# Softmax maxima carried in two extra rows of the turned queries instead of a second accumulated matmul per score tile

## Chip, cores and metric

The kernel runs on one core of a Trainium2 chip. Its time is the device time of one execution in microseconds (us). The runs of the kernel before are given with their median, and one more execution was taken with the hardware profiler, which is where all rows below come from.

## What is computed

A two-layer network on 8 sequences of 256 tokens with 128 channels, in six stages: a mixture of 64 experts, an attention of 16 heads with 8 channels each (the first attention), the mixture again, a mixture of 8 experts, an attention of 16 heads with 64 channels, and that mixture again. Each stage normalises its input and adds its result to the residual. Only the first attention is changed. For a sequence of n = 256 tokens and 16 heads it is

```
q, k, v = split(x @ w_qkv.T + b_qkv)            # 16 heads, D = 8
q, k    = rope(elu(q) + 1), rope(elu(k) + 1)
attn    = softmax(einsum('bhnd,bhmd->bhnm', q, k) / sqrt(D), axis=-1)
out     = einsum('bhnm,bhmd->bhnd', attn, v) + depthwise_conv3(v)
```

## The kernel before

The stage is the function attention_zero (L1645 to L2197). Each engine has its own instruction list, which it works off in order; semaphores tie them together. TensorE is called PE here, VectorE DVE, ScalarE ACT, GpSimd POOL.

**Layout.** Queries and keys of a sequence are stacked by tokens (stack, L1687): for every head a strip of HW = 32 columns, of which PARTS = 24 hold the 8 channels three times, in parts (high, high, rest for q; high, rest, high for k), so that one product of 24 rows gives the score nearly in full precision; the other 8 are zero. PE turns the stack (turn_stack, L1901), four heads to 128 partitions, and ACT copies it to turned (take_stack, L2056): head h lies in partitions 32*(h%4) and up.

**Two products of the same scores.** scores_by_query (L1940) gives a head's scores with queries on partitions, in bank 0 or 1, and DVE reduces them to negated maxima (maximum, L2123). scores_by_key (L1961) gives the same scores with keys on partitions, in banks 2 to 5, two heads at a time, and ACT takes their exponential (probabilities, L2072), which the product with the values needs in this layout (values, L1984, 16 matmuls L1997 for four heads). A softmax's maximum belongs to a query, which here lies along the free dimension, so it can't be a bias of ACT. Before, it is added by PE: each score tile is accumulated from a product of 24 rows (L1974) and a second one of 32 rows in bf16 (L1980), of shift, which holds the turned maxima of all heads in two bf16 parts, with select, a matrix of ones and zeros that picks the head's two rows.

**The maxima's way.** split_maxima (L2131) writes the 16 maxima of each of the two token tiles in two bf16 parts, four times over (mparts, 128 columns for a token tile); turn_maxima (L1952) turns them with 2 bf16 transposes (L1956) into bank T = 7; take_shift (L2141) copies them (L2145) to shift.

**Order of work.** The loops run over steps n = 8*i + u, i the sequence, u = 0 to 7. Step n multiplies by key the heads 2u and 2u+1 of sequence i, and multiplies by query two heads that come 11 steps later (units, L1751): the maxima of sequence i+1 are complete at u = 4, split at u = 5, turned at u = 6 and copied at u = 7. PE's order in a step (L2009 to L2039): scores_by_key; the first of the two heads by query; at odd n the values, at even n turn_out (L2001); at u = 0 values_and_convolution of the next sequence (L1918); at u = 1 to 4 one turn_stack; at u = 6 turn_maxima; at u = 7 project of sequence i+4 (L1884, only while i+4 < 8); the second head by query. So PE meets at each border of steps a block of 12 matmuls: 2 by query (the second head of the step before), 8 by key, 2 by query. DVE's order (L2175 to L2195): at u = 5 split_maxima, at u = 1 add_convolution, at u = 7 take_shift; the first maximum; at u = 0 elus (L2109); finish (even n) or take_out (odd n); the second maximum. A product by query waits for the maximum two heads back, as only two banks serve it.

**Bank T** is shared: turn_stack, turn_maxima, project and values_and_convolution take turns in it, each waiting until the one before has been read (claim, L1879). project of u = 7 waits for take_shift of u = 7; values_and_convolution at u = 0 waits for elus, which waits for ACT's exponentials of project's result.

```
1959:             release[T] = (shift_ready, b + 1)
```

Of the kernel before, what the change touches and what calls it, by code (L numbers as in the profile page):

```python
# [14 lines left out]
BF16 = mybir.dt.bfloat16  # L15
# [8 lines left out]
P = 128  # L24
BATCH = 8
SEQ = 256
# [1618 lines left out]
def attention_zero(core, name, ctx, w):  # L1645
# [9 lines left out]
    HW = 32  # L1655
    PARTS = 3 * D0
    STEPS = H0 // 2
# [23 lines left out]
    head = sb("head", [P, H0], BF16)  # L1681
    select = sb("select", [P, H0, P], BF16)
# [8 lines left out]
    mparts = sb("mparts", [P, 2, 4, 2 * H0], BF16)  # L1691
    shift = [sb(f"shift{i}", [P, SEQ], BF16) for i in range(2)]
# [12 lines left out]
    head_ready = sem("head_ready")  # L1705
    rows_done = sem("rows_done")
    rows_ready = sem("rows_ready")
    select_ready = sem("select_ready")
# [81 lines left out]
    def stacks(eng, b, step):  # L1790
        s = b % 2
        q, k = (stack[s][:, a, :, :, :].rearrange("p t h d -> p (t h) d") for a in range(2))
        for a, m in enumerate((q, k)):
            full = z[s][:, 2 * a:2 * a + 2, :].rearrange("p t (h d) -> p (t h) d", d=D0)

            view = m[:, :, 0:PARTS].rearrange("p n (i d) -> p n i d", d=D0)
# [3 lines left out]
        for a, m in enumerate((q, k)):  # L1800
            full = z[s][:, 2 * a:2 * a + 2, :].rearrange("p t (h d) -> p (t h) d", d=D0)
            at = 2 * D0 if a == 0 else D0
            last = rest_part(eng, m[:, :, at:at + D0], full, m[:, :, 0:D0])
        return last

    def gpsimd(pool):
# [16 lines left out]
        for m in stack:  # L1823
            pool.memset(m[:, :, :, :, PARTS:HW].rearrange("p a t h d -> p (a t h) d"), 0.0).then_inc(filled, 1)
        step(pool.memset(head[:, :], 0.0))

        for part in range(2):
            ins = pool.affine_select(out=head[:, :].rearrange("p (g j) -> p g j", j=HG),
                                     in_=head[:, :].rearrange("p (g j) -> p g j", j=HG), compare_op=ALU.not_equal,
                                     fill=1.0, base=-H0 * part, pattern=[[-HG, GROUPS], [-HW - 1, HG]],  # L1830
                                     channel_multiplier=1)
            if part == 0:
                step(ins)
        ins.then_inc(head_ready, 1)
# [41 lines left out]
    def tensor(pe):  # L1876
# [24 lines left out]
        def turn_stack(b, v):  # L1901
# [4 lines left out]
            if b == 0 and v == 0:  # L1906
                pe.wait_ge(filled, 3)
# [10 lines left out]
        def values_and_convolution(b):  # L1918
            i = value_bank(b)
            claim(i)  # L1920
            if b == 0:
                pe.wait_ge(v_prep_ready, 1)
                pe.wait_ge(filled, 5)
# [16 lines left out]
        def scores_by_query(b, h):  # L1940
            n, g, rows = b * H0 + h, h // HG, slice(HW * (h % HG), HW * (h % HG) + PARTS)
# [10 lines left out]
        def turn_maxima(b):  # L1952
            claim(T)
            pe.wait_ge(parts_ready, b + 1)
            for t in range(2):
                last = pe.transpose(bank[T].bitcast(BF16)[:, P * t:P * t + P],  # L1956
                                    mparts[:, t, :, :].rearrange("p i h -> p (i h)"), core.identb[:, :])
# [3 lines left out]
        def scores_by_key(b, u):  # L1961
            m = b * STEPS + u
            if m == 0:
                pe.wait_ge(select_ready, 1)
# [790 lines left out]
```

## Time and profile before

| | us |
|---|---|
| median of 3 runs | 1109.68 |
| lowest and highest | 1099.80, 1115.09 |
| the profiled execution, its own time | 1098.92 |
| its span in the profile | 1097.2 |

The span runs from the first to the last instruction of the core; the execution's own time is 1.7 us longer. The profile lists for each engine how long it was busy, and a granted clock of TensorE of 1.0 (2.4 GHz) or 0.5 (1.2 GHz) by stretch. In the timeline, instructions of one line that follow each other closely are merged ("x2"), and the time in brackets is the engine's idle time before, with what ended it. A matmul's recorded duration holds its latency, so successive starts, not durations, tell its pace. The first attention lies between 133.7 and 335 us.

### The profile page before, as it was taken

The numbers are of one execution on the slowest core, as the hardware profiler recorded it, in microseconds if no ns is written. First come the engines' busy times: TensorE is split into PE (matmuls) and PEld (weight loads), VectorE is DVE, ScalarE is ACT, GpSimd is POOL, SyncE is SP. The second block draws the span as 40 slices with busy tenths as digits, with TensorE's granted clock in tenths as the row PEclk, the third lists the DMA queues.
The fourth block names the chain that finished last, engine by engine and source line by source line (L and its number), as shares of the span: only waits on it lengthen the run. The fifth ranks groups of instructions, "written<-read, shape, count | busy, mean of one in ns | idle before, by whom it ended". The sixth has DMA issues, their size and how long they took to land.

```text
span 1097.2 us, 23131 instructions
## 1 busy us (share of the span) xinstructions
PE 914.0 (83%) x7238; PEld 688.1 (63%) x7242; DVE 757.6 (69%) x2659; ACT 534.7 (49%) x1489; POOL 272.2 (25%) x349
## 2 busy tenths in 40 slices
PE   5899758999996899937997289999999999658992
PEld 4466646666764456836896166666666766437992
DVE  7767885787868766885555557677677667674555
ACT  4222132665664232034454258677778668523553
POOL 1012183323101004047744410000000000067642
PEclk9999965999996999957999589999999999958997
DMA  9031099600006212083311175534643541253303
GB/s 243 19 98 34 16 364 328 206 2 1 1 2 169 55 41 90 1 249 99 106 42 40 56 211 174 149 113 125 193 116 98 174 135 59 62 153 92 91 32 118
DMA packets 134947, 119.47 MB, mean 109 GB/s; under 512 B 11011, under 2 KB 115227, under 8 KB 134836
## 3 DMA queue, kind: packets, MB, share of 16 engines
q1 hardware_dynamic: 130292, 109.57, 33.9%
q0 software_dynamic: 4544, 8.54, 2.4%
q8 instruction: 55, 0.90, 0.3%
q14 instruction: 56, 0.46, 0.1%
HBM read 67.19 MB, written 51.80 MB: 108 GB/s over the span
## 4 chain that ended last, share of the span: by engine, by line
PE 58%; DVE 21%; issue 9%; DMA 3%; ACT 3%; POOL 3%; SPq 1%; DVEq 1%; POOLq 0%; ACTq 0%
PE psum L802 5%; PE psum L1374 5%; PE psum L1292 4%; PE psum L811 4%; PE psum L1948 4%; PE psum L1997 3%; PE psum L590 3%; PE psum L2418 3%; PE psum L2463 3%; PE psum L2430 2%; DVE a_L L2588 2%; PE psum L592 2%; PE psum L591 2%; DVE a_G L2507 2%; PE psum L1912 2%
## 5 line engine op out<-in xcount | busy, mean ns | idle before, releaser
L2128 DVE TENSOR_REDUCE a_negmax<-psum 128x2 f32<-128x512 f32 x128 | 84.4, 687 | 36.4 <-PE psum L1948 35.6
L2077 ACT ACTIVATE a_PT<-psum 128x1024 f32<-128x1024 f32 x64 | 65.6, 1025 | 28.5 <-PE psum L1980 28.3
L2534 ACT ACTIVATE a_pr<-a_L,a_least 128x128 f32<-128x128 f32 x128 | 50.8, 397 | 54.1 <-DVE a_least L2588 54.1
L857 ACT ACTIVATE f_hT<-psum,f_wt 128x128 f32<-128x128 f32 x156 | 44.7, 369 | 46.8 <-PE psum L802 46.8
L857 ACT ACTIVATE g_hT<-psum,g_wt 128x128 f32<-128x128 f32 x156 | 44.5, 370 | 44.7 <-PE psum L802 40.9
L1948 PE MATMUL psum<-a_turned 24*128 24x256 f32 x256 | 59.3, 355 | 5.7 <-DVE a_negmax L2128 5.7
L2536 ACT ACTIVATE a_pr<-a_L,a_least 128x256 f32<-128x256 f32 x128 | 63.7, 498 | 0.0
L2418 PE MATMUL psum<-a_KT,a_Q 64*128 64x128 f32 (+1 forms) x512 | 59.7, 351 | 1.4 <-DVE a_least L2588 1.4
L2453 PEld LDWEIGHTS psum<-a_PT,a_V 128*64 128x64 f32 x512 | 31.0, 136 | 40.9 <-issue 16.8
L2544 ACT ACTIVATE a_PT<-psum 128x384 f32<-128x384 f32 x128 | 55.6, 489 | 1.9 <-PE psum L2430 1.7
L2430 PE MATMUL psum<-ident,a_pr 128*128 128x128 f32 x384 | 53.6, 276 | 2.9 <-DVE a_pr L2354 2.6
L2453 PE MATMUL psum<-a_PT,a_V 128*64 128x256 f32 (+1 forms) x512 | 55.5, 338 | 0.0
L2588 DVE CUSTOM_DVE_ANT_0 a_L<-psum,a_X 128x256 f32<-128x256 f32 x128 | 53.8, 421 | 0.0
L1974 PE MATMUL psum<-a_turned 24*128 24x256 f32 x256 | 53.0, 349 | 0.0
L1948 PEld LDWEIGHTS psum<-a_turned 24*128 24x128 f32 x256 | 39.1, 203 | 21.0 <-DVE a_negmax L2128 10.1
L576 POOL CAST a_xs_high<-a_xnT 128x256 fp32r<-128x256 f32 x8 | 3.3, 417 | 194.4 <-PE psum L592 194.4
L946 DVE COPY g_wt<-g_w_all 128x1156 f32 x39 | 29.9, 769 | 30.6 <-DVE g_y L940 27.0
L946 DVE COPY f_wt<-f_w_all 128x1156 f32 x39 | 30.6, 786 | 28.8 <-DVE f_y L940 25.4
L2586 DVE CUSTOM_DVE_ANT_0 a_L<-psum,a_X 128x128 f32<-128x128 f32 x128 | 36.7, 286 | 18.5 <-PE psum L2418 18.5
L2430 PEld LDWEIGHTS psum<-ident,a_pr 128*128 128x128 f32 x384 | 44.3, 141 | 7.8 <-issue 2.7
L802 PE MATMUL psum<-f_xT,f_wt 128*128 128x128 f32 x312 | 47.3, 298 | 1.3
L743 POOL DMA_INDIRECT g_back_dram<-g_y,g_xin x39 | 40.1, 1029 | 32.3 <-DVE g_y L940 28.5
(574 smaller groups left out, 2687.6 us busy)
## 6 DMA issues: line engine op xcount, KB each, us to landing
z<-a_G SPq DMA_DIRECT2D x32, 512.0 KB, 2.9
a_X<-z SPq DMA_DIRECT2D x16, 1024.0 KB, 7.0
f_slots_dram<-empty SPq DMA_DIRECT2D x1, 8910.0 KB, 27.1
g_slots_dram<-empty SPq DMA_DIRECT2D x1, 8910.0 KB, 51.1
a_X<-z SPq DMA_DIRECT2D x16, 512.0 KB, 3.9
f_wgu<-in_gate_up SPq DMA_DIRECT2D x16, 384.0 KB, 6.3
z<-pad SPq DMA_DIRECT2D x6, 1024.0 KB, 10.3
g_wgu<-in_gate_up SPq DMA_DIRECT2D x16, 384.0 KB, 7.0
```

The source lines that it names most:

```text
L802: last = pe.matmul(bank[i % 2][:, P * c:P * c + P], wt[i % WBUF][:, P * c:P * c + P], xT[:, i % 2, :], start=True, stop=True)
L857: act.activation(hT[:, i % 2, c, :], bank[i % 2][:, P * c:P * c + P], ACT.Relu, bias=wt[i % WBUF][:, B1 + c:B1 + c + 1]).then_inc(relu_don ...
L946: dve.tensor_copy(wt[i % WBUF][:, :], w_all[:, ds(e, 1), :].rearrange("p a n -> p (a n)")).then_inc(copied, 1)
L1948: last = pe.matmul(bank[h % 2][:, SEQ * t:SEQ * t + SEQ], q[rows, g, P * t:P * t + P].bitcast(F32R), k[rows, g, :].bitcast(F32R), start=Tr ...
L2077: act.activation(PT[m % 4][:, :, :, :].rearrange("p j t n -> p j (t n)"), core.psum[:, 2 + 2 * (u % 2):4 + 2 * (u % 2), :], ACT.Exp, scale ...
L2128: dve.tensor_reduce(negmax[:, :, h], bank[h % 2].rearrange("p (t n) -> p t n", n=SEQ), AX.X, ALU.max, negate=True).then_inc(max_done, 1)
L2418: last = pe.matmul(out, Q[s][rows, c, queries], KT[s][rows, c, keys], start=True, stop=True)
L2430: last = pe.transpose(bank[2 + i][:, P * j:P * j + P], pr[:, n % SLOTS, P * j:P * j + P], core.ident[:, :])
L2453: last = pe.matmul(o[D1 * i:D1 * i + D1, queries], V[s][:, kt, D1 * h:D1 * h + D1], PT[:, (2 * m + i) % TSLOTS, keys], start=(kt == 0), st ...
L2536: act.activation(pr[:, o, P:3 * P], L[:, o, P:3 * P], ACT.Exp, bias=least[:, o, 1:2], scale=-1.0, accum_out=sums[:, o, 1:2]).then_inc(p_re ...
L2544: act.activation(PT[:, n % TSLOTS, :], bank[2 + n % 2][:, 0:3 * P], ACT.Copy).then_inc(pT_ready, 1)
L2588: dve.tensor_tensor_reduce(L[:, o, P:3 * P], S[:, P:3 * P], X1[s][:, h, :], 1.0, 3.0e38, ALU.add, ALU.min, least[:, o, 1:2]).then_inc(l_re ...
```

## The change

The strip of a head gets two rows ahead of its 24: USED = OWN + PARTS = 26 of 32. In the keys they are ones, in the queries zeros, so that the product by query is what it was. When the maxima are known they are turned to where each head's two rows lie, with zeros elsewhere, and added in place to the turned queries; the product by key then holds them, and the second accumulation goes, with select, shift and the head pattern they were made from. mparts grows to four groups of 128 columns, turn_maxima to 8 transposes, and take_shift becomes an addition over 4 groups of 256 columns.

```diff
@@ -1652,8 +1652,10 @@
     bank = core.bank
     SCALE = float(1.0 / np.sqrt(D0))
-    HW = 32
+    HW, OWN = 32, 2
     PARTS = 3 * D0
+    USED = OWN + PARTS
     STEPS = H0 // 2
     GROUPS = H0 // HG
...
@@ -1688,8 +1688,8 @@
     turned = [[sb(f"turned{i}{a}", [P, GROUPS, SEQ]) for a in range(2)] for i in range(NT)]
     Vs = [sb(f"Vs{i}", [P, 2, H0, VW]) for i in range(NT)]
     negmax = sb("negmax", [P, 2, H0])
-    mparts = sb("mparts", [P, 2, 4, 2 * H0], BF16)
-    shift = [sb(f"shift{i}", [P, SEQ], BF16) for i in range(2)]
+    mparts = sb("mparts", [P, 2, GROUPS, HG * HW], BF16)
     PT = [sb(f"PT{i}", [P, 2, 2, SEQ]) for i in range(4)]
     OT = [sb(f"OT{i}", [P, SEQ]) for i in range(2)]
     rden = sb("rden", [P, 2, HG])
...
@@ -1793,14 +1792,14 @@
-            view = m[:, :, 0:PARTS].rearrange("p n (i d) -> p n i d", d=D0)
+            view = m[:, :, OWN:USED].rearrange("p n (i d) -> p n i d", d=D0)
...
-            last = rest_part(eng, m[:, :, at:at + D0], full, m[:, :, 0:D0])
+            last = rest_part(eng, m[:, :, OWN + at:OWN + at + D0], full, m[:, :, OWN:OWN + D0])
...
@@ -1821,17 +1820,10 @@
         pool.memset(ones_f[:, :], 1.0).then_inc(diag_ready, 1)
         pool.memset(ln.xnT[:, :, 0:SEQ + 2:SEQ + 1], 0.0).then_inc(filled, 1)
         for m in stack:
-            pool.memset(m[:, :, :, :, PARTS:HW].rearrange("p a t h d -> p (a t h) d"), 0.0).then_inc(filled, 1)
-        step(pool.memset(head[:, :], 0.0))
-
-        for part in range(2):
-            ins = pool.affine_select(out=head[:, :].rearrange("p (g j) -> p g j", j=HG),
-                                     in_=head[:, :].rearrange("p (g j) -> p g j", j=HG), compare_op=ALU.not_equal,
-                                     fill=1.0, base=-H0 * part, pattern=[[-HG, GROUPS], [-HW - 1, HG]],
-                                     channel_multiplier=1)
-            if part == 0:
-                step(ins)
-        ins.then_inc(head_ready, 1)
+            for a, ones in enumerate((0.0, 1.0)):
+                pool.memset(m[:, a, :, :, 0:OWN].rearrange("p t h d -> p (t h) d"), ones).then_inc(filled, 1)
+            pool.memset(m[:, :, :, :, USED:HW].rearrange("p a t h d -> p (a t h) d"), 0.0).then_inc(filled, 1)
+        pool.memset(mparts[:, :, :, :], 0.0).then_inc(mparts_filled, 1)
         pool.wait_ge(bias_loaded, 16)
         step(pool.tensor_copy(bias[:, 0:2, :], bqkv[:, 0:2, :]))
         split_bias(0, 2, qk_bias_ready)
...
@@ -1938,7 +1930,7 @@
             release[i] = (l_added, b + 1)
         def scores_by_query(b, h):
-            n, g, rows = b * H0 + h, h // HG, slice(HW * (h % HG), HW * (h % HG) + PARTS)
+            n, g, rows = b * H0 + h, h // HG, slice(HW * (h % HG), HW * (h % HG) + USED)
             if h % (2 * HG) == 0:
                 pe.wait_ge(tk_ready, 4 * b + 2 * (h // (2 * HG)) + 2)
             if n >= 2:
...
@@ -1952,16 +1944,15 @@
         def turn_maxima(b):
             claim(T)
             pe.wait_ge(parts_ready, b + 1)
-            for t in range(2):
-                last = pe.transpose(bank[T].bitcast(BF16)[:, P * t:P * t + P],
-                                    mparts[:, t, :, :].rearrange("p i h -> p (i h)"), core.identb[:, :])
+            for g in range(GROUPS):
+                for t in range(2):
+                    last = pe.transpose(bank[T].bitcast(BF16)[:, SEQ * g + P * t:SEQ * g + P * t + P], mparts[:, t, g, :],
+                                        core.identb[:, :])
             last.then_inc(parts_turned, 1)
             release[T] = (shift_ready, b + 1)
         def scores_by_key(b, u):
             m = b * STEPS + u
-            if m == 0:
-                pe.wait_ge(select_ready, 1)
             if u == 0:
                 pe.wait_ge(shift_ready, b + 1)
             if m >= 2:
...
@@ -1970,15 +1961,10 @@
             for t in range(2):
                 for j in range(2):
                     h = 2 * u + j
-                    rows = slice(HW * (h % HG), HW * (h % HG) + PARTS)
-                    pe.matmul(bank[2 + 2 * (u % 2) + j][:, SEQ * t:SEQ * t + SEQ],
-                              k[rows, h // HG, P * t:P * t + P].bitcast(F32R), q[rows, h // HG, :].bitcast(F32R),
-                              start=True, stop=False, skip_group_check=True)
-                for j in range(2):
-                    h = 2 * u + j
-                    rows = slice(HW * (h % HG), HW * (h % HG) + HW)
-                    last = pe.matmul(bank[2 + 2 * (u % 2) + j][:, SEQ * t:SEQ * t + SEQ], select[rows, h, :],
-                                     shift[b % 2][rows, :], start=False, stop=True, skip_group_check=True)
+                    rows = slice(HW * (h % HG), HW * (h % HG) + USED)
+                    last = pe.matmul(bank[2 + 2 * (u % 2) + j][:, SEQ * t:SEQ * t + SEQ],
+                                     k[rows, h // HG, P * t:P * t + P].bitcast(F32R), q[rows, h // HG, :].bitcast(F32R),
+                                     start=True, stop=True, skip_group_check=True)
             last.then_inc(s2_done, 1)
         def values(m):
...
@@ -2079,8 +2065,6 @@
         ln.deviation(act)
         act.activation(ln.unused[:, 1:2], core.ones[:, 0:1], ACT.Exp)
-        act.wait_ge(head_ready, 1)
-        copy(select[:, :, :], bcast(head[:, :], P)).then_inc(select_ready, 1)
         ln.take_quarter(act, 0)
         for n in range(FIRST, END):
             i, u = place(n)
...
@@ -2132,17 +2116,19 @@
             dve.wait_ge(max_done, H0 * (b + 1))
             if b:
                 dve.wait_ge(parts_turned, b)
-            full = negmax[:, :, :].unsqueeze(2).to_broadcast([P, 2, 4, H0])
-            dve.tensor_copy(mparts[:, :, :, 0:H0], full).then_inc(hi_ready, 1)
+            else:
+                dve.wait_ge(mparts_filled, 1)
+            own = mparts[:, :, :, :].rearrange("p t g (j c) -> p t (g j) c", c=HW)
+            dve.tensor_copy(own[:, :, :, 0], negmax[:, :, :]).then_inc(hi_ready, 1)
             dve.wait_ge(hi_ready, b + 1)
-            dve.tensor_tensor(mparts[:, :, :, H0:2 * H0], full, mparts[:, :, :, 0:H0],
-                              ALU.subtract).then_inc(parts_ready, 1)
+            dve.tensor_tensor(own[:, :, :, 1], negmax[:, :, :], own[:, :, :, 0], ALU.subtract).then_inc(parts_ready, 1)
         def take_shift(b):
             dve.wait_ge(parts_turned, b + 1)
-            if b >= 2:
-                dve.wait_ge(s2_done, STEPS * (b - 1))
-            dve.tensor_copy(shift[b % 2][:, :], bank[T].bitcast(BF16)[:, 0:SEQ]).then_inc(shift_ready, 1)
+            q = turned[b % NT][0]
+            dve.tensor_tensor(q[:, :, :].bitcast(F32R), q[:, :, :], bank[T].bitcast(BF16).rearrange("p (g n) -> p g n", n=SEQ),
+                              ALU.add).then_inc(shift_ready, 1)
         def add_convolution(b):
```

The waits for filled count the four more memsets, and the declarations of head, select and their semaphores go.

## Rows read from the trace of the kernel before

**Rows 1.** The page: busy time, share of the span, instructions.
```profile
PE 914.0 (83%) x7238; PEld 688.1 (63%) x7242; DVE 757.6 (69%) x2659; ACT 534.7 (49%) x1489; POOL 272.2 (25%) x349
```

**Rows 2.** Stretches of the first attention: us, each engine's busy time, granted clock, DMA.
```profile
227.24:232.08 4.84, 3.73 (x32) 3.14 (x31) 3.25 (x6) 2.14 (x3) 2.34 (x3) 1.00 0.00 0
232.08:238.81 6.73, 6.73 (x84) 4.57 (x83) 5.43 (x12) 4.55 (x6) 4.42 (x6) 1.00 0.02 5
...
227.24:247.60 20.36, 19.25 (x209) 14.01 (x208) 16.17 (x37) 11.88 (x15) 6.76 (x8) 1.00 0.01 2
```

**Rows 3.** Timeline of PE from block of step 5: start, us, idle before.
```profile
240.53 0.38 PE L1948 MATMUL psum<-a_turned 24*128 24x256 f32 x1
...
241.45 1.07 PE L1997 MATMUL psum<-a_PT,a_Vs 128*32 128x256 f32 x16
242.45 0.38 PE L1948 MATMUL psum<-a_turned 24*128 24x256 f32 x1
...
243.31 0.50 PE L1948 MATMUL psum<-a_turned 24*128 24x256 f32 x2
...
244.02 0.27 PE L1956 MATMUL psum<-identb,a_mparts 128*128 128x128 bf16 x2
```

**Rows 4.** Timeline of DVE over steps 4 to 7 of the same sequence.
```profile
239.35 1.29 DVE L2128 TENSOR_REDUCE a_negmax<-psum 128x2 f32<-128x512 f32 x2 [0.56 <-PE psum L1948]
...
245.94 0.28 DVE L2145 COPY a_shift<-psum 128x256 bf16<-128x256 bf16 x1
...
246.73 0.42 DVE L2158 COPY a_OT<-psum 128x256 f32<-128x256 f32 x1
```

**Rows 5.** Timeline of PE and DVE across the end of that sequence.
```profile
246.31 0.70 PE L1894 MATMUL psum<-a_wqkv,a_xnT 128*128 128x256 f32 x2
...
247.60 0.38 PE L1948 MATMUL psum<-a_turned 24*128 24x256 f32 x1
...
248.14 1.29 DVE L2128 TENSOR_REDUCE a_negmax<-psum 128x2 f32<-128x512 f32 x2 [0.99 <-PE psum L1948]
...
249.34 0.68 DVE L2114 SCALAR_TENSOR_TENSOR a_elu<-psum,a_e 128x512 f32<-128x512 f32 x1
...
250.08 0.70 PE L1928 MATMUL psum<-a_wv,a_xnT 128*128 128x256 f32 x2 [1.12 <-DVE a_elu L2114]
```

**Rows 6.** Groups by line and shape, 140 to 330 us: busy us, mean ns, idle before.
```profile
L1980 PE MATMUL psum<-a_shift,a_select 32*128 32x256 bf16 x256 | 46.5, 282 | 0.0
...
L2138 DVE TENSOR_TENSOR a_mparts<-a_negmax,a_mparts 128x128 bf16<-128x128 f32 x8 | 2.3, 292 | 0.3
...
L2136 DVE CAST a_mparts<-a_negmax 128x128 bf16<-128x128 f32 x8 | 1.8, 227 | 0.3
```

**Rows 7.** Timeline of the last steps, without products by query: PE.
```profile
326.39 0.38 PE L1974 MATMUL psum<-a_turned 24*128 24x256 f32 x2
...
326.62 0.28 PE L1980 MATMUL psum<-a_shift,a_select 32*128 32x256 bf16 x2
...
326.87 0.28 PE L1980 MATMUL psum<-a_shift,a_select 32*128 32x256 bf16 x2
...
329.17 0.38 PE L1974 MATMUL psum<-a_turned 24*128 24x256 f32 x2
```

**Rows 8.** Single lines: durations in ns min/median/max, first and last start, shapes.
```profile
L2151 DVE TENSOR_TENSOR x<-x,psum x8: 410/410/414, 181.5 to 309.5; 128x256 f32<-128x256 f32 x8
...
L2114 DVE SCALAR_TENSOR_TENSOR a_elu<-psum,a_e x8: 678/682/692, 146.8 to 269.7; 128x512 f32<-128x512 f32 x8
...
L1788 POOL TENSOR_TENSOR a_z<-a_z,a_rot x6: 1270/1281/1282, 170.4 to 273.4; 128x512 f32<-128x512 f32 x6
```

**Rows 9.** Timeline ahead of the first block by key: PE's project.
```profile
183.36 0.70 PE L1894 MATMUL psum<-a_wqkv,a_xnT 128*128 128x256 f32 x2 [0.30 <-DVE a_shift L2145]
```

**Rows 10.** Stretches: the first block by key up to the next, and the stage after.
```profile
184.80:191.88 7.08, 5.66 (x29) 4.83 (x28) 1.98 (x3) 2.25 (x3) 3.86 (x4) 0.54 0.58 198
191.30:338.00 146.70, 136.43 (x1526) 97.03 (x1525) 111.15 (x276) 86.29 (x104) 32.88 (x43) 1.00 0.14 42
```

## What the change does to the time, predicted before it was run

> **What bounds the kernel now.** The page comes first: PE is the busiest engine over the whole span, DVE the second [rows 1]. That average covers six stages, and only the first attention changes, so the next view is the stretches of that stage. It is periodic: one sequence of eight steps takes 20.36 us, of which PE is busy 19.25 and DVE 16.17 [rows 2]. The reader should see two kinds of stretch in it. From the block of step 1 (232.08) to that of step 4 (238.81) PE is busy 6.73 of 6.73 us and DVE 5.43: PE sets the pace. From step 0 to step 1 PE is busy only 3.73 of 4.84 us [rows 2]. The third view, DVE's timeline, tells what happens between: from 239.35 DVE works without a gap until the end of the copy that starts at 246.73 and takes 0.42, so for 7.8 us DVE sets the pace [rows 4]. PE's timeline agrees: the block of step 6 starts at 242.45, and its last pair by query only at 243.31, having waited for a maximum [rows 3]. Last, the end of a sequence: project at 246.31, right behind take_shift (245.94 + 0.28 = 246.22) [rows 4, 5]; the block of step 0 at 247.60; DVE's maximum at 248.14 after 0.99 us of idleness; elus at 249.34; values_and_convolution at 250.08, for which PE idled 1.12 us [rows 5].
>
> So a sequence is a ring of four parts: PE's steps 1 to 3; DVE from step 4 to take_shift; project and the block of step 0; the wait for elus and values_and_convolution. A saving counts only in the part whose engine sets the pace.
>
> **Removed: four bf16 matmuls per step**, 256 in all [rows 6]. Their mean of 282 ns is latency, not pace. A block of twelve matmuls takes 0.92 us from its first start to the next operation (240.53 to 241.45) [rows 3]. In the last steps, which have no product by query, a pair of 24-row products plus a pair of bf16 ones takes 0.25 us (bf16 start at 326.62 to the next bf16 start at 326.87) [rows 7]. Both kinds stream 256 columns, so about half of it, 0.11 to 0.12, belongs to the bf16 pair. A block has two such pairs: 0.22 us less, leaving 0.70. Bounds: nothing, if the other row groups' streams keep the block as long, and 0.31, if a third of it goes as four of twelve instructions. I take 0.22, as the two rows in the last steps measure the pair itself.
>
> In steps 1 to 3 that is 3 x 0.22 = 0.66 us, if DVE keeps up. DVE idles 0.56 us once in two steps (the bracket at 239.35) [rows 4], and two steps would lose 0.44. That nearly exhausts its slack, and the second step of a pair will sometimes wait. I take 0.5 us per sequence. In steps 4 to 7 DVE sets the pace: nothing. In step 0 the maximum comes 0.54 us after the block starts, from its first two matmuls (247.60 to 248.14) [rows 5], and then DVE's two maxima and elus follow each other: nothing.
>
> **Moved and grown: take_shift.** The copy of 256 columns took 0.28 us [rows 4]. It becomes an fp32 addition of 1024 columns, one operand from PSUM. Not in the trace; the nearest rows are the DVE operations with one PSUM and one SBUF operand: 410 ns for 256 columns, 682 for 512 [rows 8]. That is 1.0625 ns a column, hence 682 + 512 x 1.0625 = 1226 ns, 0.94 more. Bounds: 0.68 in all, if it took no longer than 512 columns do; 2.55, if it ran at POOL's 1.28 us per 512 [rows 8]. I take 1.23, the straight line through DVE's own rows.
>
> **Split of the maxima.** A cast of 227 ns and a subtraction of 292 over 128 columns [rows 6] become the same over 32 columns. Estimate: 0.15 + 0.20, 0.17 us less; bounds 0 and 0.25. It is in DVE's unbroken stretch, so it counts.
>
> **Turning.** Eight transposes instead of two. The two take 0.27 us and one lasts 0.22 (mean pace 0.05 to 0.06) [rows 3], so six more cost PE 0.33 us at step 6. There PE waits for DVE (0.86 us into its block at 243.31) [rows 3], which hides them. If that cover were gone, they would cost 0.33 per sequence.
>
> **The wait that grows.** project claims bank T and may start only when take_shift has read it. take_shift would end at 246.22 - 0.17 + 0.94 = 246.99, project at about 247.05 instead of 246.31: 0.75 us later [rows 4, 5]. Behind it in PE's order stand the last product by query and the block of step 0; DVE's maxima, elus and values_and_convolution wait for these. ACT's exponentials too are 0.75 later, in step with the rest. On DVE the maximum and take_out behind take_shift (1.0 us) fall into the idle 0.99 us before 248.14, which moves along with PE [rows 5].
>
> **The rest.** ACT's copy of select goes, once, at the start, where ACT waits for PE's transposes right after: nothing. POOL's extra memsets replace two selects and have slack: nothing, at most 0.5. Waits on shift buffers go; they weren't late.
>
> **The sum**, against the profiled execution's own time of 1098.92 us:
> - sequences 0 to 3 (with project): -0.5 + 0.75 = +0.25 each, +1.0.
> - sequences 4 to 6: no project, but take_shift still stands ahead of the maximum that frees a bank; +0.2 each, +0.6.
> - before the first block by key: project already waits there for take_shift (0.30 us) [rows 9], so +0.94, and 0.1 for transposes at the low clock: +1.0.
> - the last eleven steps have no maxima. Two take 2.78 us (326.39 to 329.17) [rows 7]; the blocks give 0.5, but values, DVE's copy, turning back and DVE's division, which share one bank, need almost as long. I take 0.15 per pair, -0.6 with the odd ends; bounds -0.2 and -2.5.
>
> Together +2.0 us: 1100.9 on the profiled execution's scale. The median of the runs shown stands 10.8 us above that execution, so the forecast for a median is 1109.7 + 2.0 = 1111.7 us. A measurement of this kernel tells about 2% (22 us) from no change, and all of this is far below.
>
> **Rivals.**
> 1. PE sets the pace throughout. For it: PE busy 19.25 of 20.36 us [rows 2]. Against it: DVE's 7.8 us without a gap [rows 4]. It gives 64 x 0.22 = 14.1 less and 7 x 0.33 = 2.3 more: -11.8, 1097.9 us. Chance 0.15.
> 2. The addition is much dearer than the line through DVE's rows. At the upper bound of 2.55 it costs 1.32 more on each of 8 turns: 1111.7 + 10.6 = 1122.3 us. For it: a bf16 PSUM operand mixed with an fp32 one is in no row. Against it: no DVE row is that slow per column. Chance 0.1.
> 3. The removal doesn't do what it says: the bf16 pairs stream beside products of other row groups and the block keeps nearly 0.92. Then the 0.5 per sequence doesn't come: 6 sequences x 0.5 = 3.0 more, 1114.7 us. For it: the block overlaps four row groups already, twelve matmuls in 0.92 us [rows 3]. Chance 0.1.
> 4. Slower, by the clock. PE gets idler: 0.75 us more before project, shortly before its idle 1.12 us [rows 5]. If the granted clock falls at each end of a sequence, that stretch costs what it did the first time, at a mean clock of 0.54: 7.08 us instead of 4.84 [rows 2, 10], 2.24 each. With seven sequences: +15.7, 1127.4 us. It decides from the point where the two idle stretches together look to the chip like those before 191 us. Against it: from 191.3 to 338 us the clock stayed at 1.00, through idle stretches of 1.12 us [rows 5, 10]. Chance 0.1.
>
> On the fourth, the Trainium skill, "TensorE: Matmul & The Clock Gate", section "Part 4: PE-mode transpose", says that transposes don't count as PE activity for the clock as other matmuls do. This change removes counted matmuls and adds transposes, so by that page its chance would be higher. The trace speaks against a large effect: the clock was full through stretches with many transposes.
>
> **Chances.** The forecast has 0.5, the four rivals 0.15, 0.1, 0.1, 0.1, and 0.05 is left for what I don't see. The range takes in the first three rivals, and the spread of the runs before: 1097 to 1124 us. The fourth lies outside. Faster by over 2% needs more than all the PE work removed: 0.02. Slower by over 2% needs the clock to fall and the addition to be dear as well: 0.04. Within 2%: 0.94.
>
> **What would show it.** Right: in the profile after, the addition at about 1.23 us; the block near 0.70 us; project waiting about 0.8 us for take_shift; the last steps slightly shorter; a sequence of 20.4 to 20.8 us; DVE's busy time up by some 6 us in the stage and PE's down by about 10. Wrong: a sequence under 20 us (rival 1), the addition above 1.5 us (rival 2), the block still near 0.9 (rival 3), a granted clock of 0.5 between 191 and 338 us (rival 4).

## The result, and the profile after

| | before | after |
|---|---|---|
| median of 20 executions, us | 1105.14 | 1113.89 |
| lowest and highest | 1096.34, 1115.73 | 1107.84, 1117.69 |
| mean | 1106.5 | 1113.4 |
| the profiled execution, own time | 1098.92 | 1112.25 |

The ratio after to before is 1.0096, with a 95% interval of 1.0069 to 1.0124; this ratio and those below leave out executions more than 1.5% above the fastest of their kernel. Over all 20 executions of each, the means differ by 6.9 us (0.6%) and the medians by 8.7. So the kernel got slower by 0.6 to 1%. The forecast of 1111.7 us lies 2.2 us below the median, but its step was +2.0 us.

The three runs known before hid a pattern. Of the 20 executions before, ten lie at 1096.3 to 1100.7 us and ten at 1109.6 to 1115.7, with nothing between. Of the 20 after, none is below 1107.8. The profile before is of the lower group.

The page after, to set beside [rows 1]:

```profile
PE 920.4 (83%) x7030; PEld 689.2 (62%) x7034; DVE 765.2 (69%) x2659; ACT 531.6 (48%) x1488; POOL 273.2 (25%) x351
```

PE has 208 instructions fewer (256 removed, 48 added) and is nevertheless busy 6.4 us longer. Fewer instructions that are busy for longer are the first sign of the clock. The stretches of the first attention, with the granted clock in the third place from the end, answer to [rows 2, 10]:

```profile
184.40:194.60 10.20, 8.59 (x36) 7.11 (x37) 2.49 (x5) 2.52 (x4) 4.77 (x6) 0.50 0.70 227
...
198.10:215.20 17.10, 17.10 (x114) 10.98 (x112) 10.89 (x23) 7.05 (x9) 0.00 (x0) 0.50 0.77 231
...
218.60:222.00 3.40, 3.40 (x18) 3.10 (x16) 0.76 (x1) 0.00 (x0) 3.32 (x4) 0.50 0.02 5
222.00:297.10 75.10, 66.86 (x688) 47.80 (x692) 62.35 (x139) 44.22 (x57) 23.07 (x29) 1.00 0.01 1
297.10:303.90 6.80, 6.80 (x38) 5.25 (x31) 4.31 (x9) 1.78 (x2) 0.00 (x0) 0.50 0.02 4
...
237.82:258.55 20.73, 18.11 (x184) 12.99 (x184) 17.03 (x37) 11.78 (x15) 6.75 (x8) 1.00 0.01 2
```

Before, PE ran at 2.4 GHz from 191.3 to 338 us without a break [rows 10]. After, it is at 1.2 GHz until 194.6, again from 198.1 for 17.1 us, and twice more. At full clock (last row) a sequence takes 20.73 us instead of 20.36; PE is busy 18.11 of it instead of 19.25 and DVE 17.03 instead of 16.17 [rows 2].

That gives a balance, from the starts of ACT's 64 exponentials. The first and the last, before (L2077) and after (L2063):

```profile
186.53 1.02 ACT L2077 ACTIVATE a_PT<-psum 128x1024 f32<-128x1024 f32 x1 [0.36 <-PE psum L1980]
...
329.96 1.02 ACT L2077 ACTIVATE a_PT<-psum 128x1024 f32<-128x1024 f32 x1
...
188.16 1.01 ACT L2063 ACTIVATE a_PT<-psum 128x1024 f32<-128x1024 f32 x1
...
343.60 1.03 ACT L2063 ACTIVATE a_PT<-psum 128x1024 f32<-128x1024 f32 x1
```

The last one starts 13.6 us later than before. The first starts 1.6 later; the sequences 2, 3, 4 and 6, without a fall of the clock, take 0.37, 0.37, 0.35 and 0.36 us more; sequences 0, 1 and 5, with falls, take 7.0, 1.9 and 2.1 more; the last steps take 0.5 less. Sum: 13.6. If the three had cost 0.37 each, 3.7 us would be left. So between these two executions **3.7 us is the ring of waits, and 9.9 us is the clock that fell where it had not fallen before**. The 3.7 hold some more of the clock: the 1.6 us at the start include 1.0 that project lost by running at 1.2 GHz. Against the kernel before as a whole the clock's share is smaller, because the profile before is of the group that kept its clock: if the 3.7 us hold in the means too, 3.2 of their difference of 6.9 are left for the clock (an estimate).

The ring looks as the prediction drew it. DVE's timeline over steps 5 to 7, to [rows 4]:

```profile
231.22 0.24 DVE L2122 CAST a_mparts<-a_negmax 128x32 bf16<-128x32 f32 x1
231.49 0.30 DVE L2124 TENSOR_TENSOR a_mparts<-a_negmax,a_mparts 128x32 bf16<-128x32 f32 x1
...
235.26 1.21 DVE L2130 TENSOR_TENSOR a_turned<-a_turned,psum 128x1024 fp32r<-128x1024 f32 x1
```

PE's, of the same sequence, to [rows 3, 5]:

```profile
233.34 0.61 PE L1949 MATMUL psum<-identb,a_mparts 128*128 128x128 bf16 x8
...
236.52 0.70 PE L1886 MATMUL psum<-a_wqkv,a_xnT 128*128 128x256 f32 x2 [0.82 <-DVE a_turned L2130]
...
237.82 0.38 PE L1940 MATMUL psum<-a_turned 26*128 26x256 f32 x1
...
238.48 0.44 PE L1990 MATMUL psum<-ident,a_OT 128*128 128x128 f32 x2
...
240.29 0.70 PE L1920 MATMUL psum<-a_wv,a_xnT 128*128 128x256 f32 x2 [1.38 <-DVE a_elu L2098]
```

The addition lasts 1.21 us. project starts 0.05 after its end, having waited 0.82 us. The block of step 0 takes 0.66 (237.82 to 238.48), where the block of [rows 3] took 0.92. And before values_and_convolution PE idles 1.38 us instead of 1.12: the quarter of a microsecond that the block lost went into the wait, as forecast for step 0.

### The profile page after: what moved, and what is told of

Same layout as the page of the kernel before. It is cut to its first block, busy times and chain, and to the rows that moved or that the text cites. A ratio compares the mean times of both kernels' runs of the same rounds, so it can differ in the third digit from the quotient of the medians.

```text
span 1110.4 us, 22707 instructions
## 1 busy us (share of the span) xinstructions
PE 920.4 (83%) x7030; PEld 689.2 (62%) x7034; DVE 765.2 (69%) x2659; ACT 531.6 (48%) x1488; POOL 273.2 (25%) x351
## 4 chain that ended last, share of the span: by engine, by line
PE 55%; DVE 25%; issue 9%; DMA 3%; ACT 3%; DVEq 2%; SPq 1%; POOL 1%; POOLq 0%; ACTq 0%
PE psum L802 6%; PE psum L1374 5%; PE psum L811 4%; PE psum L1292 4%; PE psum L2404 3%; PE psum L590 3%; PE psum L2449 3%; PE psum L1940 3%; DVE a_negmax L2112 2%; PE psum L2416 2%; PE psum L1983 2%; DVE a_L L2574 2%; PE psum L592 2%; PE psum L591 2%; DVE a_G L2493 1%
## 5 line engine op out<-in xcount | busy, mean ns | idle before, releaser
L2063 ACT ACTIVATE a_PT<-psum 128x1024 f32<-128x1024 f32 x64 | 65.2, 1023 | 28.4 <-PE psum L1965 27.7
L1940 PE MATMUL psum<-a_turned 26*128 26x256 f32 x256 | 52.3, 372 | 7.6 <-DVE a_negmax L2112 7.3
L1940 PEld LDWEIGHTS psum<-a_turned 26*128 26x128 f32 x256 | 33.2, 216 | 25.1 <-DVE a_negmax L2112 18.5
L743 POOL DMA_INDIRECT f_back_dram<-f_y,f_xin x39 | 40.5, 1039 | 30.4 <-DVE f_y L940 25.7
L1965 PE MATMUL psum<-a_turned 26*128 26x256 f32 x256 | 47.3, 323 | 0.5 <-DVE a_turned L2130 0.4
```

The lines of the kernel that those rows point to most:

```text
L743: pool.indirect_dma_start(back_dram[:, :], bass.IndirectOffsetOnAxis(ap=xin[:, i, P:P + 1].bitcast(I32), axis=0), y[i % YBUF][:, :], None, ...
L1940: last = pe.matmul(bank[h % 2][:, SEQ * t:SEQ * t + SEQ], q[rows, g, P * t:P * t + P].bitcast(F32R), k[rows, g, :].bitcast(F32R), start=Tr ...
L2063: act.activation(PT[m % 4][:, :, :, :].rearrange("p j t n -> p j (t n)"), core.psum[:, 2 + 2 * (u % 2):4 + 2 * (u % 2), :], ACT.Exp, scale ...
```

## Experiments

Two theories. **Ring**: the loss is the longer chain DVE, project, DVE, values. **Clock**: PE, with less to do and more to wait for, is granted 1.2 GHz more often, and most of the loss is that. Beside each kernel stand 29 executions of the kernel before on the same chip. The chips differ: means of the kernel before are 1140.4 us (first chip), 1141.5 (second) and 1107.7 (third), so each kernel is read against its own. Means here are over all executions, and the clock is the granted clock of an execution, averaged over them. The standard error of a difference between two of these means is 1.4 to 2.5 us. Each kernel has one profile, of one of its executions.

| kernel | chip | executions | mean us | against before | mean clock | full-clock sequence us |
|---|---|---|---|---|---|---|
| before | first | 29 | 1140.4 | | 0.891 | 20.36 |
| no_second | first | 12 | 1149.5 | +9.1 | 0.878 | 19.81 |
| long_shift | first | 6 | 1154.1 | +13.8 | 0.887 | 21.6 |
| filler | first | 12 | 1144.8 | +4.4 | 0.890 | 20.73 |
| early_add | first | 12 | 1146.9 | +6.5 | 0.883 | 20.13 |
| before | second | 29 | 1141.5 | | 0.890 | 20.36 |
| changed_again | second | 6 | 1153.0 | +11.5 | 0.879 | 20.73 |
| zero_pairs | second | 12 | 1146.2 | +4.8 | 0.892 | 21.29 |
| before_filler | second | 12 | 1138.3 | -3.2 | 0.893 | 20.36 |
| by_query_first | second | 12 | 1145.5 | +4.0 | 0.885 | 19.89 |
| before | third | 29 | 1107.7 | | 0.896 | 20.36 |
| before_reordered | third | 12 | 1103.5 | -4.2 | 0.901 | 20.29 |
| changed_padded | third | 12 | 1107.2 | -0.5 | 0.900 | 20.07 |
| changed_unpadded | third | 12 | 1104.4 | -3.4 | 0.900 | 19.91 |

The sequence is the time between exponentials of two sequences' same step, where the clock was full between; for the kernel before it is from its one profile.

### The removal alone: no_second

```diff
-                              start=True, stop=False, skip_group_check=True)
-                for j in range(2):
...
-                    last = pe.matmul(bank[2 + 2 * (u % 2) + j][:, SEQ * t:SEQ * t + SEQ], select[rows, h, :],
-                                     shift[b % 2][rows, :], start=False, stop=True, skip_group_check=True)
+                              start=True, stop=True, skip_group_check=True)
```

> The kernel before without its 256 bf16 matmuls; all else stays, the copy of the turned maxima too, so the scores by key are not lowered by their maxima. It is the removal alone. Theory 'ring': blocks of 0.68 us instead of 0.92, but only the three blocks of steps 1 to 3 count: 0.4 to 0.5 us less per sequence, 2 to 4 us less in all against the kernel before. Theory 'clock': the same shortening, but with less for PE to do the granted clock falls in early sequences in more of the executions, so the median comes out 0 to 6 us above the kernel before, at a mean clock of 0.89 to 0.90.

Measured: ratio 1.0073 (1.0027 to 1.012). From the exponential of one step 1 to the next it takes 19.81 us instead of 20.36, so the ring got 0.55 us shorter, a little more than the 0.4 to 0.5 expected. Yet the kernel is 9.1 us slower in the mean and 15.0 in the median, more than even theory clock gave. Its twelve executions lie at 1144.3 to 1153.6 us, at clocks of 0.875 to 0.883. The kernel before on this chip has 17 at 1132.9 to 1138.4 (clock 0.889 to 0.903) and 12 at 1147.1 to 1150.0 (0.879 to 0.886). The stretches of no_second:

```profile
198.80:215.90 17.10, 17.10 (x109) 10.61 (x108) 10.09 (x23) 7.20 (x9) 0.00 (x0) 0.50 0.87 264
...
253.40:267.10 13.70, 12.77 (x65) 9.21 (x67) 6.56 (x15) 3.58 (x6) 4.68 (x5) 0.50 0.00 0
...
297.80:308.00 10.20, 10.20 (x61) 7.75 (x61) 5.34 (x14) 2.61 (x4) 0.00 (x0) 0.50 0.00 1
```

Work was only taken away, nothing put on DVE, no wait added, and the kernel lost time at the lower clock. Theory ring can't give that.

### DVE's part alone: long_shift

```diff
         def take_shift(b):
...
+            dve.tensor_tensor(spare[:, :, :].bitcast(F32R), turned[b % NT][0][:, :, :],
+                              bank[T].bitcast(BF16)[:, 0:SEQ].unsqueeze(1).to_broadcast([P, GROUPS, SEQ]), ALU.add)
             dve.tensor_copy(shift[b % 2][:, :], bank[T].bitcast(BF16)[:, 0:SEQ]).then_inc(shift_ready, 1)
```

> The kernel before with one more DVE addition of 1024 fp32 columns ahead of take_shift's copy, its result unused: DVE's part of the change alone (1.13 us more per sequence, where the change has 0.93), with all matmuls kept. Theory 'ring': project starts 1.1 us later, each sequence about 1.05 us longer, 7 to 8.5 us in all. Theory 'clock': the same plus a fall of the granted clock in early sequences, 12 to 18 us in all.

Measured: ratio 1.0104 (1.0034 to 1.0174), +13.8 in the mean, in the range of theory clock, at a mean clock of 0.887 against 0.891. A sequence grew by 1.28 us (21.64), somewhat more than expected. PE's timeline has the wait:

```profile
239.66 0.70 PE L1895 MATMUL psum<-a_wqkv,a_xnT 128*128 128x256 f32 x2 [1.03 <-DVE a_shift L2148]
```

So DVE's work ahead of project does pass into the ring nearly whole, as the prediction had it. In the profile the clock fell to 1.2 GHz for 20.5 us here too, though all PE work was kept:

```profile
199.20:219.70 20.50, 20.50 (x135) 13.12 (x134) 11.76 (x25) 7.98 (x10) 0.00 (x0) 0.50 0.64 193
```

But this run doesn't separate the theories. The interval, 4 to 20 us, also holds what theory ring gives for 1.28 us in each of seven sequences, 9 us. And the profile is of the slowest of the six (clock 0.877); the other five have 0.885 to 0.891, inside the range of the kernel before. That an added wait alone lets the clock fall is not shown.

### Work put back where it isn't needed: zero_pairs, beside changed_again

changed_again is the changed kernel, unedited. zero_pairs:

```diff
...
+                for j in range(2):
+                    h = 2 * u + j
+                    rows = slice(HW * (h % HG), HW * (h % HG) + HW)
+                    last = pe.matmul(bank[2 + 2 * (u % 2) + j][:, SEQ * t:SEQ * t + SEQ], zeros[rows, 0:P],
+                                     zeros[rows, :], start=False, stop=True, skip_group_check=True)
```

> The changed kernel as it is, beside the runs of the kernel before on the same chip as the three that follow. Both theories: about 1% above the kernel before in the mean; sequences of 20.72 us where the clock is full. Theory 'clock': executions of the kernel before fall in two clusters 13 to 15 us apart, by their mean granted clock, and those of the changed kernel all lie at a clock as low as the upper cluster's. Theory 'ring': the changed kernel shows the same two clusters, each some 4 us up.

> The changed kernel with the 256 bf16 matmuls put back at their old places, of the same shape, multiplying zeros, so that they add nothing to the scores. PE has the work of before and DVE that of the change. Theory 'ring': strictly more work than the changed kernel: blocks of 0.92 us again, some 0.5 us more per sequence, 3 to 4 us above the changed kernel. Theory 'clock', in the form that the removal of PE work lets the clock fall: mean granted clock higher by 0.005 to 0.01 than the changed kernel's, and the time equal to or 2 to 8 us below it, in spite of the added work.

Measured: changed_again 1.012 (1.0054 to 1.0186), zero_pairs 1.0044 (1.0004 to 1.0085). zero_pairs does all that the changed kernel does and 256 matmuls more. At full clock its sequence is 0.56 us longer, as theory ring says. It is 6.8 us faster in the mean (standard error 2.1; changed_again has only six executions), at a clock of 0.892 against 0.879. Its executions lie at 1143.8 to 1149.0, those of changed_again at 1147.8 to 1160.9. The stretches of changed_again:

```profile
185.50:195.70 10.20, 8.65 (x37) 7.17 (x38) 2.32 (x4) 2.52 (x4) 4.97 (x6) 0.50 0.70 225
...
199.10:216.20 17.10, 17.10 (x114) 10.98 (x112) 10.85 (x23) 7.00 (x9) 0.00 (x0) 0.50 0.77 230
...
298.10:304.90 6.80, 6.80 (x39) 5.25 (x31) 4.28 (x9) 1.75 (x2) 0.00 (x0) 0.50 0.01 4
```

And those of zero_pairs, whose first falls end at 196.8 us and which then has one short one:

```profile
186.60:196.80 10.20, 8.78 (x41) 7.23 (x40) 2.23 (x4) 2.63 (x4) 5.01 (x6) 0.50 0.71 227
196.80:258.30 61.50, 55.59 (x613) 40.19 (x610) 50.14 (x107) 35.18 (x44) 16.15 (x20) 1.00 0.27 79
258.30:261.70 3.40, 3.40 (x19) 3.10 (x18) 0.40 (x1) 0.39 (x1) 3.26 (x5) 0.50 0.00 0
```

changed_again repeats the falls of the first profile on another chip, nearly to the microsecond, so they aren't an accident of one execution. It is the fastest of its six; the others, up to 13 us longer at clocks down to 0.869, have no profile. In the profile of zero_pairs the long fall is gone. The two kernels differ only in unneeded work, and the one with more is faster at a higher clock. Theory ring had it 3 to 4 us slower. Measured against the 6.9 us of the changed kernel's first 20 executions instead of the 11.5, zero_pairs still stands 2 us lower, not 3 to 4 higher. So putting the matmuls back wins more by the clock than it costs in the ring. The second half of what was expected of changed_again by theory clock holds too: no execution at the lower group's clock of 0.894 to 0.900. The first half, "about 1%", was 1.2%.

### Idle stretches filled: filler and before_filler

```diff
+        def filler(n, first, many):
+            if n < 0:
+                claim(first)
+            else:
+                pe.wait_ge(p_ready, n)
+            for _ in range(many):
+                pe.matmul(bank[first], ones_f[:, :].bitcast(F32R), bias_rows[:, 0:4, :].bitcast(F32R), start=True,
+                          stop=True, skip_group_check=True)
...
+            if 0 <= n and value_step(n) is not None:
+                filler(n, 4, 4)
             if value_step(n) is not None:
                 values_and_convolution(value_step(n))
...
+            if -1 <= n and u == 7 and inside(i + 4):
+                filler(n, 2, 3)
             if u == 7 and inside(i + 4):
                 project(i + 4)
```

before_filler has the first call only, with 5 matmuls, in the kernel before.

> The changed kernel, with extra matmuls whose results nobody reads, issued by PE just where it would idle: 3 of 512 columns ahead of project at each step 7, 4 ahead of values_and_convolution at each step 0, from the first block by key on. They add nothing to the work that is used. Theory 'clock' (about 4 us of the change's loss is the ring of waits, the rest is a granted clock that falls in the first two sequences because PE idles more): the clock stays up more often, the mean granted clock of a run rises from 0.89 towards 0.91, and the time falls by 5 to 10 us below the changed kernel's. Theory 'ring' (the whole loss is the longer chain DVE, project, DVE, values): the time stays within 2 us of the changed kernel's, or rises by 1 to 2 us where a filler runs over.

> The kernel before with 5 unread matmuls of 512 columns at each step 0, where PE idles 1.12 us before values_and_convolution; nothing else. Theory 'ring': the same time or up to 1 us more. Theory 'clock': the cluster of slow executions (mean clock 0.88, 14 us longer) gets rarer or goes, and the mean falls by 3 to 6 us, the lowest execution staying within 1 us.

Measured: filler 1.0058 (1.0018 to 1.0099), before_filler 0.9988 (0.9948 to 1.0027). The cleaner of the two is before_filler. Its ratio doesn't tell it from the kernel before; the distribution of its executions does. Of 29 executions of the kernel before, 15 lie at 1132.4 to 1136.8 and 14 at 1146.9 to 1152.2. With the fillers the twelve lie at 1136.6 to 1140.2: the upper group is gone, and the mean is 3.2 us lower for more work. Against what was expected, the lowest rose by 4.2 us instead of 1. PE's timeline shows the fillers fit (the product behind them starts without a wait):

```profile
230.43 1.41 PE L2014 MATMUL psum<-a_bias_rows,a_ones_f 128*128 128x512 f32 x5
231.79 0.70 PE L1928 MATMUL psum<-a_wv,a_xnT 128*128 128x256 f32 x2
```

but only while there are elus to wait for. Sequences 5 and 6, which have none, took 18.92 and 15.94 us instead of 17.76 and 14.77, 2.3 us together for nothing.

filler, on the changed kernel, has fillers at the same two places and still stands only 4.4 us above its kernel before, where the changed kernel stands 6.9 and 11.5 above on its two chips. It ran on another chip than changed_again, so its gain is less sure. It fell short of what theory clock gave: the clock did not rise towards 0.91 but stayed at 0.890, and the gain is 2.5 or 7 us, by which of the two it is set against, where 5 to 10 were expected. In its profile, of its fastest execution, the clock stays up from 192.8 to 308.9 us, and sequence 0 takes 22.05 us instead of 28.6:

```profile
192.80:308.90 116.10, 110.42 (x1067) 78.98 (x1069) 94.11 (x208) 66.48 (x85) 31.47 (x38) 1.00 0.17 51
```

### Shorter rings: early_add and by_query_first

```diff
-            if u == 7 and inside(i + 1):
-                take_shift(i + 1)
...
+            if u == 6 and inside(i + 1):
+                take_shift(i + 1)
             if due[1]:
                 maximum(*due[1])
```

> The changed kernel, with take_shift moved on DVE from the head of step 7 to ahead of the second maximum of step 6, so that one maximum of 0.60 us no longer stands between the turned maxima and the release of bank T. Theory 'ring': each sequence with project gets 0.5 to 0.6 us shorter (20.72 to about 20.15), those without somewhat less, 3 to 4 us in all against the changed kernel. Theory 'clock': the same 3 to 4 us, and if the idle time before project is what lets the clock fall, 5 us or more on top, as the mean granted clock rises above 0.90.

by_query_first adds to that, on PE:

```diff
+            if 0 <= n and u == 0 and due[1]:
+                scores_by_query(*due[1])
             if value_step(n) is not None:
                 values_and_convolution(value_step(n))
...
-            if due[1]:
+            if due[1] and not (0 <= n and u == 0):
                 scores_by_query(*due[1])
```

> early_add, and at step 0 the second head's product by query goes ahead of values_and_convolution instead of behind it, so that PE does it in its idle 1.38 us and DVE reduces it while PE is at the convolution. Both theories: a sequence shorter by 0.2 to 0.4 us than early_add's 20.13. Theory 'ring': 1.5 to 3 us below early_add in all. Theory 'clock': PE's idle stretch is cut by 0.4 us, so the clock falls a little less often, and the time is 3 us or more below early_add's.

Measured: early_add 1.0051 (1.0003 to 1.0099), by_query_first 1.0063 (1.0025 to 1.0101). Both shorten the ring as worked out: 20.13 us (0.60 less, by the one maximum that no longer stands in the way) and 19.89 (0.24 less). In early_add the addition ends at 246.29 and project waits 0.23 instead of 0.82:

```profile
245.08 1.21 DVE L2130 TENSOR_TENSOR a_turned<-a_turned,psum 128x1024 fp32r<-128x1024 f32 x1
...
246.35 0.70 PE L1886 MATMUL psum<-a_wqkv,a_xnT 128*128 128x256 f32 x2 [0.23 <-DVE a_turned L2130]
```

Both rings are shorter than that of the kernel before, and both kernels are slower than it, at clocks of 0.883 and 0.885. Two of early_add's twelve, the profiled one among them, kept a clock of 0.891 and 0.894 and took 1137 to 1138 us; the other ten took 1145 to 1156. by_query_first stands 2.5 us lower against its own kernel before than early_add does, within the 1.5 to 3 of theory ring and short of the 3 or more of theory clock. The further hope of theory clock, that the idle time ahead of project is what lets the clock fall, didn't come true: most of it went, and the clock stayed at 0.883. A shorter ring for the same work doesn't by itself keep the clock up. zero_pairs, with the pairs of zeros, held 0.892 and filler 0.890, the level of the kernel before.

### A version that beats both?

before_reordered is the kernel before with the order of by_query_first at step 0 and 1 + 3 fillers around it, only for sequences 0 to 4. changed_unpadded is by_query_first with the same fillers. changed_padded has the pairs of zeros as well, only at steps 5, 6, 7 and 0.

```diff
+            if 0 <= n and u == 0 and i + 3 < BATCH:
+                filler(n, 4, 1)
             if 0 <= n and u == 0 and due[1]:
                 scores_by_query(*due[1])
+            if 0 <= n and u == 0 and i + 3 < BATCH:
+                filler(n, 4, 3)
...
```

> The kernel before with two edits at step 0 of sequences 0 to 4, where PE idles 1.12 us: the second product by query goes ahead of values_and_convolution (as in by_query_first), and 1 + 3 unread matmuls of 512 columns fill most of the rest; no fillers where there are no elus (before_filler had them there too, and its sequences 5 and 6 grew by 1.1 us each). Theory 'clock': no slow cluster, all executions within some 5 us, the mean 5 to 7 us below the mean of the kernel before, and the lowest executions 1 to 2 us below its lowest by the reordering (0.2 to 0.3 us a sequence). Theory 'ring' alone: both clusters stay, each 1 to 2 us lower.

> The changed kernel with the addition early, the second product by query first at step 0, the same 1 + 3 fillers at step 0 of sequences 0 to 4, and the bf16 matmuls with zeros put back only at steps 5, 6, 7 and 0 of sequences 0 to 6, where DVE sets the pace. Theory 'clock': the pairs are nearly free there (sequences within 0.2 us of by_query_first's 19.9) and the clock stays up as in the kernel before: 4 to 8 us below the mean of the kernel before. Theory 'ring' alone: the time of by_query_first, 4 us above the mean of the kernel before.

> changed_padded without the bf16 matmuls with zeros: addition early, second product by query first, fillers at step 0. It tells the pairs of zeros at DVE's steps from the fillers at step 0. Theory 'clock': the filled idle stretch alone brings back part of it: mean granted clock between by_query_first's and changed_padded's, and the time 2 to 4 us above changed_padded. Theory 'ring' alone: 0 to 1 us below changed_padded, as it has less work.

Measured: ratios 0.9994 (0.9954 to 1.0034), 0.998 (0.9932 to 1.0028) and 1.0009 (0.9965 to 1.0053). None is told from the kernel before by its interval. Over all executions before_reordered is 4.2 us below its mean and at most 1107.2 us, where 16 of the 29 of the kernel before are above 1108.9. changed_unpadded is 3.4 below in the mean, changed_padded 0.5. So the change can be kept at no loss, with the addition early, the order of step 0 turned and its idle time filled, but it brings nothing over the same fillers without it. Of what was expected, before_reordered came near: no execution in the upper group but two levels still, its mean 4.2 below and not 5 to 7, its lowest no lower (1098.7 against 1098.2). changed_padded missed its 4 to 8 us: two of its twelve lie at 1116.5. changed_unpadded was expected 2 to 4 us above changed_padded and came out 2.9 below, with a standard error of 1.7: the pairs of zeros show no gain once the fillers are there (clocks of 0.900 and 0.900), and cost 0.16 us per sequence. The reordering in the kernel before gave 0.07 us per sequence, not 0.2 to 0.3.

## Why the prediction was right and wrong

- **The number**: near the median by luck. The base was the median of three executions, 1109.7 us, 4.5 above the 1105.1 of twenty, which fall in two groups; the step was 6.7 too small, +2.0 instead of +8.7. The two errors nearly cancel.
- **Which engine sets the pace where**: right. A block shrank by 0.26 us (0.22 was taken). In a whole sequence the removal alone gives 0.55 (0.5 was taken), not the 8 x 0.22 of rival 1.
- **The addition**: 1.21 us measured, 1.23 forecast.
- **The split of the maxima**: wrong. The cast takes 0.24 us and the subtraction 0.30 for 32 columns, as long as for 128 [rows 6]. The forecast had 0.17 less. So project came not 0.75 but about 0.93 later. Less the 0.55 of the removal that is 0.38, which is what sequences 2 and 3 grew by (0.37) where 0.25 was forecast.
- **The six more transposes**: right, hidden at step 6; eight take 0.54 us to the next block (233.34 to 233.88).
- **The first block**: forecast +1.0, measured +1.6. project waits 1.23 us for the addition instead of 0.30 [rows 9], the 0.94 forecast. But it then runs behind 184.4 us, where the clock falls in both profiles, and so at 1.2 GHz, from 184.46 to the block at 186.89, 2.43 us instead of the 1.44 from its start [rows 9] to the block at 184.80 [rows 10]. PE's timeline after:

```profile
184.46 1.22 PE L1886 MATMUL psum<-a_wqkv,a_xnT 128*128 128x256 f32 x2 [1.23 <-DVE a_turned L2130]
...
186.89 0.58 PE L1940 MATMUL psum<-a_turned 26*128 26x256 f32 x1
```

- **Sequences 4 to 6**: forecast +0.2 each, measured +0.35 where the clock was full. **The last steps**: forecast -0.6, measured -0.5; two steps take 2.70 us instead of 2.78 [rows 7]. PE's timeline after, two steps apart:

```profile
339.38 0.50 PE L1965 MATMUL psum<-a_turned 26*128 26x256 f32 x4
...
342.08 0.50 PE L1965 MATMUL psum<-a_turned 26*128 26x256 f32 x4
```

- **The step that failed** is the overlooked clock: the sum took the granted clock to stay at 1.00 and priced its fall at nothing, as the fourth rival, with a chance of 0.1. That rival's price was 2.24 us for each of seven sequences; in fact three sequences paid, 6.6, 1.6 and 1.7 us, 9.9 together. By the prediction's own sign, a granted clock of 0.5 between 191 and 338 us, it is what happened; and PE's busy time in the stage rose by 5 us (175.6 up to 335.2 us before, 180.6 up to 348.8 after) where a fall of 10 was given. The place was right in kind and wrong in size, because a fall near the start lasted 17.1 us and ran through steps in which PE sets the pace. The evidence against it, "from 191.3 to 338 us the clock stayed at 1.00", was one execution's. The three times given, 1099.8 to 1115.1 us, a spread of 1.4%, already said that executions differ by more than the whole forecast. They were read as noise.

With matmuls taken away the clock fell (no_second), with matmuls put back it rose (zero_pairs). The Trainium skill, "TensorE: Matmul & The Clock Gate", section "Part 4: PE-mode transpose", has matmuls count as activity and transposes not in the same way; the runs agree for matmuls, and whether transposes count, no run here tells.

Not settled: where the clock falls in the upper group of executions of the kernel before. Their mean clock is lower by some 0.014 (0.883 against 0.897 on the second chip), but no profile was taken of one. Nor is it settled which part of PE's work holds the clock up, whether a longer wait alone, with all matmuls kept, lowers it (long_shift doesn't decide it), or whether a mere shift of the stage in time would (no run has only that).

## What to carry to other kernels

A saving on the busiest engine is worth something only in the stretches where that engine sets the pace; elsewhere it turns into waiting, and on TensorE fewer matmuls can cost clock on top. Before pricing a change that takes matmuls away, look at the spread of the times: here two groups of executions, 14 us apart at clocks of 0.897 and 0.883, said that the clock was near an edge, and the profile showed only one side of it. Test it by adding matmuls that nobody reads where TensorE idles: if the kernel gets faster or its spread closes, as with before_filler, the clock is what is being lost.

## What the runs showed of the hardware

- Taking 256 matmuls away made a kernel 9.1 us slower in the mean (clock 0.891 to 0.878), and putting 256 unread ones in made another 6.8 us faster (0.879 to 0.892; six executions against twelve).
- The clock fell to 1.2 GHz for 17.1, 3.4 and 6.8 us in a stage where TensorE never idled for more than 1.55 us between the first block by key and the last.
- A cast and a subtraction on DVE took 0.24 and 0.30 us for 32 bf16 columns written at a stride, no less than 0.23 and 0.29 for 128 columns side by side.
- A DVE addition of 1024 fp32 columns with one bf16 operand in PSUM took 1.21 us, on the line through 410 ns for 256 and 682 for 512.
- The falls of the granted clock lie at the same places of the stage in two profiles of one kernel from two chips (17.1 us from 198.1, and from 199.1 in a span shifted by 0.9 us), whose times differ by 3%.
